# One copy and one subtraction across two PSUM banks, in place of two of each, in an attention kernel

## The reference

```
# layer 0, one head
B, C, D = Wb @ x, Wc @ x, Wd @ x                 # (256, 1024) each
S = softmax(B^T C, axis=-1)                      # (1024, 1024)
y = gamma * (D @ S^T) + x
# layer 1, four heads of 64 channels
h = group_norm(y, 32 groups) * gn_w + gn_b
q, k, v = wq @ h + bq, wk @ h + bk, wv @ h + bv
attn = softmax(q^T k / 8, axis=-1)               # (1024, 1024) for each head
out = y + wp @ concat(attn @ v) + bp
```

## Time and profile before

| | before |
|---|---|
| median of 3 runs | 718.05 us (716.38 to 718.53) |
| the profiled execution | 718.41 us |
| its span on the core | 716.7 us |
| TensorE busy (matmuls) | 697.7 us, 97% |
| VectorE busy | 537.0 us, 75% |
| ScalarE busy | 454.7 us, 63% |
| GpSimd busy | 229.3 us, 32% |

### The profile page before, as it was taken

One profiled execution on the slowest core, in us unless ns is written; L12 is line 12 of the kernel. 1 busy time (PEld: TensorE's weight loads), 2 busy tenths in 40 slices (PEclk: granted clock), 3 DMA queues, 4 the chain that ended last, 5 costly groups with the idle time before them and its releaser, 6 DMA issues.

```text
span 716.7 us, 11880 instructions
## 1 busy us (share of the span) xinstructions
PE 697.7 (97%) x3888; PEld 592.0 (83%) x3888; DVE 537.0 (75%) x878; ACT 454.7 (63%) x820; POOL 229.3 (32%) x214
## 2 busy tenths in 40 slices
PE   4999999999999999999999999999999999999996
PEld 4888888888888887887888887887987888888885
DVE  3665455456546738999888899887889988889994
ACT  3553254245225516789777789877779878769883
POOL 0120021012003302365333356433346533334430
PEclk9999999999999999999999999999999999999999
DMA  8000220040030175500257210266401155401010
GB/s 274 5 2 29 80 67 15 29 132 0 29 110 37 45 177 124 156 1 1 75 132 174 91 38 24 56 151 148 118 15 44 44 126 124 118 16 45 16 42 32
DMA packets 29100, 52.72 MB, mean 74 GB/s; under 512 B 3456, under 2 KB 5760, under 8 KB 29056
## 3 DMA queue, kind: packets, MB, share of 16 engines
q1 hardware_dynamic: 29056, 52.19, 26.4%
HBM read 18.62 MB, written 8.39 MB: 38 GB/s over the span
## 4 chain that ended last, share of the span: by engine, by line
PE 89%; DVE 5%; ACT 3%; issue 2%; DMA 1%; SPq 0%; ACTq 0%; DVEq 0%
PE acc L1093 45%; PE scores L1093 26%; PE trans L1127 18%; DVE negmax L775 2%; DVE pt_lo L793 1%; ACT prob L582 1%; DMA x_raw<-in_x 1%; ACT pt_hi L592 1%; DVE o_sum L996 0%; ACT o_sum L696 0%; DVE x_lo L873 0%; ACT h_hi L640 0%; ACT x_hi L603 0%; DVE gn_sqdev L829 0%; DVE rsum L780 0%
## 5 line engine op out<-in xcount | busy, mean ns | idle before, releaser
L502 POOL TENSOR_SCALAR prob<-prob,rsum 128x1024 f32<-128x1024 f32 x159 | 179.3, 1127 | 470.2 <-DVE rsum L780 470.2
L592 ACT ACTIVATE pt_hi<-trans 128x512 fp32r<-128x512 f32 x320 | 174.8, 595 | 129.4 <-PE trans L1127 126.7
L775 DVE TENSOR_REDUCE negmax<-scores 128x1 f32<-128x1024 f32 x160 | 194.3, 1214 | 45.4 <-PE scores L1093 43.8
L793 DVE TENSOR_TENSOR pt_lo<-trans,pt_hi 128x512 fp32r<-128x512 f32 x320 | 204.6, 680 | 9.5 <-ACT pt_hi L592 9.3
L582 ACT ACTIVATE prob<-scores,negmax 128x1024 f32<-128x1024 f32 x160 | 179.1, 1119 | 30.0 <-DVE negmax L775 28.5
L1127 PEld LDWEIGHTS trans<-ident,prob 128*128 128x128 f32 x1280 | 147.0, 140 | 32.4 <-DVE pt_lo L793 5.4
L1127 PE MATMUL trans<-ident,prob 128*128 128x128 f32 x1280 | 168.8, 274 | 4.0 <-DVE pt_lo L793 3.4
L1093 PE MATMUL scores<-k_st,q_st 128*128 128x512 f32 x512 | 137.8, 391 | 0.0
L1093 PEld LDWEIGHTS scores<-k_st,q_st 128*128 128x128 f32 x512 | 95.9, 188 | 20.8 <-ACT prob L582 0.2
L1093 PE MATMUL acc<-pt_hi,v_st 128*128 128x512 f32 (+1 forms) x264 | 106.7, 406 | 1.9 <-DVE pt_lo L793 1.9
L1093 PE MATMUL acc<-pt_lo,v_st 128*128 128x512 f32 (+1 forms) x264 | 101.0, 385 | 0.0
(11 more groups left out here) (119 smaller groups left out, 888.2 us busy)
## 6 DMA issues: line engine op xcount, KB each, us to landing
k_st<-qk SPq DMA_DIRECT2D x64, 256.0 KB, 4.6
q_st<-qk SPq DMA_DIRECT2D x64, 128.0 KB, 2.4
x_raw<-in_x SPq DMA_DIRECT2D x8, 512.0 KB, 7.0
y_out<-in_x SPq DMA_DIRECT2D x16, 256.0 KB, 4.1
y_scratch<-y_out SPq DMA_DIRECT2D x16, 256.0 KB, 2.0
y_in<-y_scratch SPq DMA_DIRECT2D x4, 1024.0 KB, 7.4
y_res<-y_scratch SPq DMA_DIRECT2D x16, 256.0 KB, 3.5
out<-y_res SPq DMA_DIRECT2D x16, 256.0 KB, 2.1
```

The lines of the kernel that those rows point to most:

```text
L502: nc.gpsimd.tensor_scalar(p, p, rsum[:, t % 2:t % 2 + 1], 1.0, ALU.mult, ALU.mult)\
L592: nc.scalar.activation(pt_block(pt_hi, (t // 4) % 2, t, h), trans[:, h, :].rearrange("p (j n) -> p j n", n=P), ACT.Copy).then_inc(pt_high, 1)
L775: nc.vector.tensor_reduce(negmax[:, t % 2:t % 2 + 1], scores[:, t % 2, :], AX_X, ALU.max, negate=True).then_inc(max_ready, 1)
L793: nc.vector.tensor_tensor(pt_block(pt_lo, slot, t, h), trans[:, h, :].rearrange("p (j n) -> p j n", n=P), pt_block(pt_hi, slot, t, h).bitc ...
```

## The change

The two halves become one. TensorE waits once for both banks of `trans` and does the eight transposes with one signal at the end; ScalarE copies 128x1024 in one instruction that spans both banks; VectorE subtracts 128x1024 in one instruction. The semaphores still count two for a tile, so that all other waits keep their numbers.

```diff
-        def pt_block(buf, half_slot, t, h):
+        def pt_block(buf, half_slot, t):
 
-            return buf[:, half_slot, 4 * h:4 * h + 4, (t % 4) * P:(t % 4 + 1) * P]
+            return buf[:, half_slot, :, (t % 4) * P:(t % 4 + 1) * P]
+
+        def trans_keys():
+
+            return trans[:, :, :].rearrange("p h n -> p (h n)").rearrange("p (j n) -> p j n", n=P)
@@ trans_high (ScalarE)
-                for h in range(2):
-                    act.wait_ge(transposed, TRANS_CREDIT + 2 * (t0 + t) + h + 1)
-                    nc.scalar.activation(pt_block(pt_hi, (t // 4) % 2, t, h),
-                                         trans[:, h, :].rearrange("p (j n) -> p j n", n=P),
-                                         ACT.Copy).then_inc(pt_high, 1)
+                act.wait_ge(transposed, TRANS_CREDIT + 2 * (t0 + t) + 2)
+                nc.scalar.activation(pt_block(pt_hi, (t // 4) % 2, t), trans_keys(), ACT.Copy).then_inc(pt_high, 2)
@@ trans_low (VectorE)
-                for h in range(2):
-                    dve.wait_ge(pt_high, 2 * (t0 + t) + h + 1)
-                    slot = (t // 4) % 2
-                    nc.vector.tensor_tensor(pt_block(pt_lo, slot, t, h),
-                                            trans[:, h, :].rearrange("p (j n) -> p j n", n=P),
-                                            pt_block(pt_hi, slot, t, h).bitcast(F32),
-                                            ALU.subtract).then_inc(pt_split, 1)
+                dve.wait_ge(pt_high, 2 * (t0 + t) + 2)
+                slot = (t // 4) % 2
+                nc.vector.tensor_tensor(pt_block(pt_lo, slot, t), trans_keys(),
+                                        pt_block(pt_hi, slot, t).bitcast(F32), ALU.subtract).then_inc(pt_split, 2)
@@ transpose_tile (TensorE)
-                for h in range(2):
-                    pe.wait_ge(pt_split, 2 * (t0 + t) + h + 1)
-                    for b in range(4):
-                        j = 4 * h + b
-                        ins = nc.tensor.transpose(trans[:, h, b * P:(b + 1) * P],
-                                                  prob[:, t % 2, j * P:(j + 1) * P], ident[:, :])
-                    ins.then_inc(transposed, 1)
+                pe.wait_ge(pt_split, 2 * (t0 + t) + 2)
+                for j in range(NT):
+                    ins = nc.tensor.transpose(trans[:, j // 4, (j % 4) * P:(j % 4 + 1) * P],
+                                              prob[:, t % 2, j * P:(j + 1) * P], ident[:, :])
+                ins.then_inc(transposed, 2)
```

## The result

The changed kernel takes 778.86 us (median, 778.47 to 781.88) against 718.29 for the kernel before on the same chip: ratio 1.086 with an interval of 1.082 to 1.089. It is 60.6 us slower. The forecast was 768 in a range of 752 to 780, so the sign and the mechanism held and the size was 10 us short. The result lies only 1 us inside the upper end of the range.

The account below looks back on a forecast made before the run. TensorE was taken to set the time, VectorE next at 88%; short steps grow to 3.52 us, +50.1, plus 0.7 of smaller terms, rounded to +50, gives 768 us, range 752 to 780.

Parts of the forecast that it names:

- the 76 distances that were named: Layer 1, tile to tile: 58 short (under 3.1 us) and 18 medium (3.1 to 3.3) grow to 3.52, +50.1 us.
- a worked bound of 788: Total time if single copy and subtraction cost their upper bounds, making the time until trans is free 3.76 us.
- the round trip: First weight load of a tile's transposes to the next tile's, through copy and subtraction of trans: 3.52 us, bounds 3.40 to 3.76.
- this lead: Transposes that did not wait: loads run ahead (0.87 us to copy, not 0.70); a wait removes it, next long step returns it.
- the accumulation bank's waits: TensorE's wait of 0.23 us at 452.14 and two more like it go, as transposes start later: -0.7 us.
- Layer 0: Shortest distance 3.62 us at 12 places, above 3.52 by 0.1: costed at nothing, or 1.7 us at 3.76.
- The late copy after a pass of the image loop: ScalarE's late copy delays TensorE's next load: +1.0 us, less some 0.2 for a second wait that falls away.
- From the last tile's first load to the first product: End of layer 1: copy waits for eight transposes, so the first product comes at 706.07 instead of 705.48, +0.6 us.
- The granted clock at 1.00 in spite of the gaps: Changed profile: clock stays at 1.00; a fall would make the time longer than forecast.
- the other engines' loops lengthen: Rival, short steps: late row maximum delays the subtraction by 0.53 us; 808 in all 76, 781 in a third; chance 0.12.
- Partial loss: Rival: short steps beside long ones covered by their slack, only some 45 adjoining short steps lose, 752 us; chance 0.09.
- The saving of fixed cost: Rival, faster: one subtraction in place of two saves 0.08 us in 58 short steps, -4.6, 713 us; chance 0.02.

Follow-up runs that it names:

- after_pad: Changed kernel with layer 1's score product done twice in steps that have no group but av; 779.06 us.
- split_ops: Changed kernel with waits and signals once per tile, but copy and subtraction each issued as two 128x512 instructions; 779.37 us, ratio 1.086.
- sub_merged: Kernel before with only VectorE's subtraction made one of 128x1024; 750.54 us, ratio 1.045.
- copy_merged: Kernel before with only ScalarE's copy made one of 128x1024; 750.03 us, ratio 1.045.
- pe_merged: Kernel before with only TensorE's wait and signal merged, copy and subtraction left as two instructions each; 747.94 us, ratio 1.042.
- merge_long2: Kernel before with one copy and subtraction only for tiles in covered steps, TensorE in halves throughout, first image's steps 0 to 3 excluded; 717.01 us, ratio 0.9997.
- pe_unrolled: Changed kernel with TensorE's loop over layer 1's images 1 and 2 written out as straight-line code; 780.58 us, ratio 1.087.
- before_pad: Kernel before with layer 1's score product done twice in steps that have no group but av; 765.35 us.
- merge_long: Kernel before with the change, TensorE's wait included, only for tiles in steps with a projection and layer 0's longer distances; 726.42 us, ratio 1.010.

## Why the prediction was right, and where it was short

**The place and the mechanism held.** The loss lies in the 76 distances that were named, and the long steps did not grow in sum. after_pad shows that it is idle time of TensorE, split_ops that the size of the instructions is not its cause. That the time stayed inside the range has some luck in it: 780 was drawn in from a worked bound of 788, and 778.86 comes of terms that were mis-sized or not in the sum.

**The size of the round trip was the mis-sized term:** 3.52 predicted, 3.60 measured. Term by term, predicted and measured: transposes to copy 1.14 and 1.19; copy 1.10 and 1.04; hand-over to the subtraction 0.03 and 0.09; subtraction 1.21 and 1.24; hand-over to TensorE 0.05 and 0.04. The 0.03 was read from a pair of copies, where the first half's subtraction follows its copy, and a 128x1024 copy has a longer way from its recorded end to the start of what waits for it. Over 76 distances that is 76 x 0.08 = 6.1 us.

**Two more terms were missing.** In written-out code the distance is 3.66: 43 of the 76 are there, 43 x 0.06 = 2.6 us. And a short step after a long one has 3.77 in the looped images, as the loads of its transposes had run ahead:

```profile
551.64 1.03 PEld L1123 LDWEIGHTS trans<-ident,prob 128*128 128x128 f32 x8
...
555.41 0.86 PEld L1123 LDWEIGHTS trans<-ident,prob 128*128 128x128 f32 x8 [1.09 <-DVE pt_lo L793]
```

I had seen this lead and argued that it comes back in the next long step. It does, in part: those went from 4.07 to 3.93. The short and medium distances rose by 62.4 in place of 50.1, and 12.3 is 6.1 + 2.6 and 3.6 more. Of the 3.6, 3.0 are in the 18 distances that follow a long one, and 0.4 in a single distance of 4.03 in the last image, where VectorE began the subtraction 0.37 late with nothing in the profile that it waited for (split_ops has 3.66 there). The long distances then gave back 3.6, which also holds the accumulation bank's waits that I had expected to go.

**The small terms.** Layer 0 was costed at nothing behind a cover of 0.1. Its distances of 3.62 became 3.77, since there too the transposes had not waited; most came back, and 1.1 us stayed, half of it at one tile of the last image (4.10). The late copy after a pass of the image loop, priced at +0.8 in all, did not come: the copy waited there for the transposes alone and the distance is 3.77, for 3.97 before. It did come in sub_merged, at 4.77. From the last tile's first load to the first product it is 3.60 for 3.11 us, 0.5 more (0.6 was said). One term at the end I missed: the clock.

```profile
764.00:767.00 3.00, 2.96 (x17) 2.96 (x18) 0.00 (x0) 0.00 (x0) 0.00 (x0) 0.67 0.00 0
```

This is a window of the changed kernel's end; the column before the last two is the granted clock, 0.67 as a mean. From 765.10 to about 768.3 the matmuls of the epilogue start 0.21 apart and not 0.12, which is the lower level, 1.2 GHz, after TensorE had stood idle for 2.50 us before them. From that first product to the end it is 12.68 us here, 11.21 in the kernel before and 11.20 in copy_merged, which was idle for the same 2.50 us and kept its clock: it cost 1.5 us. "The granted clock at 1.00 in spite of the gaps" was thus right for the run of short steps and wrong for the end.

**The rivals.** That the other engines' loops lengthen did not happen in layer 1 of the changed kernel: the row maximum fitted in the 3.6 us. In layer 0 it happened once: in the last image two other subtractions of 0.68 us each kept VectorE until 0.27 us after the subtraction could have started, which is in the 4.10. It does show again where the round trip is 3.2 (pe_merged). Partial loss fell: short steps beside long ones lost as much as those in a row or more (3.77 for 3.60), and the long ones gave some of it back. The saving of fixed cost, the way to a faster kernel, is real in the traces as busy time (subtractions 196 us for 205) and worth nothing, also where it is covered (merge_long2).

## What to carry to other kernels

Splitting a PSUM hand-over in halves is not only about the size of instructions: it lets a buffer that is not doubled be filled and emptied at the same time. Before merging such pieces, add up the whole round trip of the buffer (fill, hand-over, each reader, hand-over) and set it against the distance at which the bound engine comes back to it; every distance below it grows to it, and one merged stage of three is enough to lose half. And check both sides of a merged tile: its wait reaches back into the step before it.

## What the runs showed of the hardware

- One copy of 128x1024 from two banks is 1.03 us and one subtraction 1.22 to 1.23, but what waits for that copy starts 0.09 to 0.10 after its end. Two copies of 128x512 with one signal at the end are 1.09 as a pair, and the waiting subtraction starts 0.03 after. From the copy's start to the subtraction's the two forms are within 0.01 us of each other (1.13 and 1.12), and the round trip was 3.60 and 3.59.
- TensorE, held by a wait, starts 0.04 us after the releasing subtraction in looped code and 0.14 after it by the chain in written-out code (a distance of 3.60 and 3.66, and of 3.66 once the loop was written out).
- The clock at the end did not follow the length of the wait alone: after 2.50 us of idle before the epilogue it fell to the lower level in the changed kernel, split_ops, after_pad and pe_unrolled and stayed at 1.00 in copy_merged; after 2.07 us it fell in sub_merged, after 2.01 it stayed in pe_merged; after 1.85 it fell in merge_long and stayed in the kernel before, before_pad and merge_long2. Each is one profiled execution, so what decides is open.
